# Moving loads, sums and logits between steps in a two-layer attention and mixture-of-experts kernel

## The reference

```python
x = x + attn_a(layernorm(x))   # 16 heads of 8, causal softmax attention
x = x + ffn(layernorm(x))      # 8 experts, top 2
x = x + attn_b(layernorm(x))   # 16 heads of 8, similarity scaled by norms, no mask
x = x + ffn(layernorm(x))      # the same expert weights again

def ffn(x):                    # 4096 tokens of 128
    logits = flat_x @ Wr                       # 128 -> 8
    top_vals, top_idx = top_k(logits, 2)
    combine = softmax(top_vals), one-hot over the experts
    h = silu(flat_x @ Wg[e]) * (flat_x @ Wu[e])   # 128 -> 512
    out = sum over e of combine[e] * (h @ Wd[e]) * 12 ** -0.5
```

## Time and profile before

| | us |
|---|---|
| three runs | 1113.69, 1089.67, 1102.22 |
| median | 1102.22 |
| the profiled execution, its own time | 1107.71 |
| its span from first to last instruction | 1105.3 |
| PE busy in the span | 993.8 (90%) |
| DVE busy | 771.1 (70%) |
| ACT busy | 712.6 (64%) |
| POOL busy | 542.9 (49%) |
| mean granted TensorE clock | 0.933 |

### The profile page before, as it was taken

One profiled execution on the slowest core, in us unless ns is written; L12 is line 12 of the kernel. 1 busy time (PEld: TensorE's weight loads), 2 busy tenths in 40 slices (PEclk: granted clock), 3 DMA queues, 4 the chain that ended last, 5 costly groups with the idle time before them and its releaser, 6 DMA issues.

```text
span 1105.3 us, 28185 instructions
## 1 busy us (share of the span) xinstructions
PE 993.8 (90%) x9148; PEld 701.1 (63%) x9148; DVE 771.1 (70%) x2335; ACT 712.6 (64%) x1399; POOL 542.9 (49%) x764
## 2 busy tenths in 40 slices
PE   2999999998988999998889899999988799999992
PEld 1345545554458999998734344445643589999992
DVE  4688878878677534465789989998687774443554
ACT  2367767765554566666558779999667555666661
POOL 3144445644650630255787846588416416204655
PEclk9999989999888999999959889999787799999996
DMA  5545766643223765675644434344321246667774
GB/s 154 115 109 126 178 163 140 163 109 95 61 69 90 185 168 146 159 185 149 173 102 110 108 91 89 90 100 97 70 61 45 77 112 176 158 148 170 190 189 140
DMA packets 239303, 139.86 MB, mean 127 GB/s; under 512 B 92724, under 2 KB 215352, under 8 KB 239160
## 3 DMA queue, kind: packets, MB, share of 16 engines
q1 hardware_dynamic: 230968, 121.29, 45.1%
q0 software_dynamic: 8192, 16.79, 5.2%
HBM read 87.86 MB, written 50.14 MB: 125 GB/s over the span
## 4 chain that ended last, share of the span: by engine, by line
PE 31%; DVE 10%; issue 4%; DMA 3%; SPq 3%; POOL 1%; ACT 1%; POOLq 0%; DVEq 0%; ACTq 0%
PE psS L364 5%; PE psO L330 4%; PE psT L1422 4%; PE psS L1415 4%; DVE mx L670 4%; PE psO L1436 2%; PE psN L1436 2%; PE psN L337 2%; DMA wuc<-in_L_ffn_Wu 1%; PE psM L285 1%; SPq L1509 1%; DMA xin<-xg 1%; DVE row L610 1%; PE psM L435 1%; PE psM L294 1%
## 5 line engine op out<-in xcount | busy, mean ns | idle before, releaser
L670 DVE TENSOR_REDUCE mx<-psS 128x3 f32<-128x384 f32 (+1 forms) x512 | 310.2, 618 | 94.2 <-PE psS L395 53.6
L364 PE MATMUL psS<-kst,qst 48*128 48x256 bf16 (+1 forms) x1024 | 196.4, 280 | 39.4 <-DVE mx L670 28.4
L567 ACT ACTIVATE pT<-psT,scb 128x512 f32<-128x512 f32 x256 | 193.3, 772 | 48.4 <-PE psT L372 45.5
L372 PE MATMUL psT<-qst,kst 50*128 50x256 bf16 (+1 forms) x1024 | 191.5, 274 | 7.2 <-DMA qst<-scr_m 4.8
L1298 POOL DMA_INDIRECT xg<-xn,slot x128 | 123.2, 962 | 127.5 <-DVE ysb L1483 75.0
L1462 ACT ACTIVATE sg<-psS 128x512 f32<-128x512 f32 x142 | 84.8, 597 | 145.3 <-PE psS L1415 142.7
L1422 PE MATMUL psT<-xTt,wuc 128*128 128x128 f32 x1136 | 155.1, 280 | 4.9 <-DMA wuc<-in_L_ffn_Wu 4.6
L562 ACT ACTIVATE pT<-psT 128x384 f32<-128x384 f32 x256 | 123.5, 488 | 55.1 <-PE psT L372 47.2
L1415 PE MATMUL psS<-xTt,wgc 128*128 128x128 f32 x1136 | 153.7, 279 | 4.2 <-DVE xTt L1475 4.2
L364 PEld LDWEIGHTS psS<-kst,qst 48*128 48x128 bf16 x1024 | 63.2, 96 | 139.0 <-DVE mx L670 72.3
L1488 DVE TENSOR_TENSOR hT<-sg,psT 128x512 f32<-128x512 f32 x142 | 97.0, 683 | 71.6 <-PE psT L1422 52.7
(11 more groups left out here) (228 smaller groups left out, 1621.4 us busy)
## 6 DMA issues: line engine op xcount, KB each, us to landing
wuc<-in_L_ffn_Wu SPq DMA_DIRECT2D x142, 256.0 KB
scr_part<-part SPq DMA_DIRECT2D x128, 128.0 KB, 2.4
qst<-scr_part SPq DMA_DIRECT2D x64, 192.0 KB, 3.6
kst<-scr_part SPq DMA_DIRECT2D x64, 192.0 KB, 4.6
eo<-ysb SPq DMA_DIRECT2D x142, 64.0 KB
xin<-xg SPq DMA_DIRECT2D x280, 32.0 KB
scr_part<-part SPq DMA_DIRECT2D x32, 192.0 KB, 2.1
xg<-zero SPq DMA_DIRECT2D x7, 576.0 KB, 3.7
```

The costliest lines, as they stand in the source:

```text
L364: return nc.tensor.matmul(ps[:, c0:c0 + n], q_[r64, t, q0], k_[r64, t, 0:n], start=(half == 0), stop=True, skip_group_check=True)
L372: return nc.tensor.matmul(ps[:, c0:c0 + T - q0], k_[m64, t, half * P:half * P + P], q_[m64, t, q0:T], start=(half == 0 or not L.causal), s ...
L567: nc.scalar.activation(pT[:, g % 8, 0:cols], psT[g % 2][:, 0:cols], ACT.Exp, scale=scb[r][:, 0, i:i + 1], bias=scb[r][:, 1, i:i + 1]).then ...
L670: nc.vector.tensor_reduce(mx3[:, u, 0:n, pos:pos + 1].rearrange("p a b -> p (a b)"), psS[h % 2][:, 0:kcols(L)].rearrange("p (a k) -> p a k ...
```

## The change

It does six things. (1) The down weights are issued in steps 3 to 10 of the attention of layer one instead of 4 to 11, the gate weights in steps 11 to 18 instead of 4 to 11, at the same points. (2) The logits of step 15 in layer two are issued as eight halves of two matmuls at heads 3 to 10 instead of four of four at heads 3 to 6, and DVE copies them at head 11 instead of 8. (3) The second half of the third sums of layer two's attention (step 6) moves from head 7 to head 5. (4) The statistics that stood at head 5 of step 6 move to head 9 of step 5. (5) The gathers of group 0 in layer one's experts are paced at two per tile instead of one and a half, as in layer two already. (6) Behind the tiles the additions start at 11, 15 and 19 tiles after `OWN + 1` instead of 13, 18 and 23 (in both layers), and the layer norm at 23 instead of 27 (layer one).

```diff
@@ -993,14 +993,15 @@
                                            xn[:, BASE[g] + 4 * i + m, :], ident[:])
             last.then_inc(r["T_ps"], 1)
 
-        def pe_logits(pe, n, i):
+        def pe_logits(pe, n, i, half=None):
             r = r_sem
             pe.wait_ge(r["T"], quads(n) + i + 1)
-            for m in range(4):
+            for m in range(4) if half is None else range(2 * half, 2 * half + 2):
                 k = 4 * i + m
                 last = nc.tensor.matmul(logit_bank(n, i)[:, E * k:E * k + E], xnT[i % 4][:, m * P:(m + 1) * P], wr[:],
                                         start=True, stop=True, skip_group_check=True)
-            last.then_inc(r["lg_ps"], 1)
+            if half is None or half:
+                last.then_inc(r["lg_ps"], 1)
 
         def pe_counts(pe, n):
 
@@ -1324,7 +1325,7 @@
                     pool.wait_ge(f_sem["u"], n0 + ROUTE_SLOT + 2 + pair // 2)
                 pool_scatter(pool, 2 * l + 1, pair)
             for pair in range(2 * SIZE[0]):
-                pool.wait_ge(f_sem["y"], n0 + OWN + (2 * pair // 3 if l == 0 else pair // 2) + 1)
+                pool.wait_ge(f_sem["y"], n0 + OWN + pair // 2 + 1)
                 pool_gather(pool, 2 * l, pair)
             for pair in range(2 * PARTS[1] if l == 1 else 0):
                 pool.wait_ge(f_sem["y"], n0 + OWN_A)
@@ -1608,12 +1609,12 @@
         def sp_beside(sp, j, point):
 
 
-            if 4 <= j < 4 + E and point == 3:
-                e = j - 4
+            if 3 <= j < 3 + E and point == 3:
+                e = j - 3
                 sp.dma_start(wd[:, e * HID:(e + 1) * HID].rearrange("p (k d) -> p k d", k=HB),
                              A["L0_ffn_Wd"][e].rearrange("(k p) d -> p k d", p=P)).then_inc(s_wffn, 16)
-            if 4 <= j < 4 + E and point == 1:
-                e = j - 4
+            if 11 <= j < 11 + E and point == 1:
+                e = j - 11
                 sp.dma_start(wg[:, e * HID:(e + 1) * HID], A["L0_ffn_Wg"][e]).then_inc(s_wg, 16)
             if j == 6:
                 if point == 0:
@@ -1670,8 +1671,8 @@
                 if l == 1 and j == 15:
                     if h == 3:
                         pe.wait_ge(L.s["oT"], 2 * (j - 4) + 2)
-                    if 3 <= h < 7:
-                        pe_logits(pe, n, h - 3)
+                    if 3 <= h < 11:
+                        pe_logits(pe, n, (h - 3) // 2, h % 2 == 0)
                     if h == 12:
                         pe.wait_ge(r_sem["lg"], LG_COPIES[n] + 1)
                 if l == 1 and j == 16 and h == 4:
@@ -1804,7 +1805,7 @@
             if (j, h) == (5, 5):
                 dve.wait_ge(r_sem["x"], 2 * (lo + 4))
                 dve_stats(lo, lo + 4)
-            if (j, h) == (6, 5):
+            if (j, h) == (5, 9):
                 dve.wait_ge(r_sem["x"], 2 * mid)
                 link(dve_stats(lo + 4, mid))
             if (j, h) == (6, 9):
@@ -1843,7 +1844,7 @@
         def dve_third_route(dve, j, h):
 
             n, size = 2, SIZE[0]
-            if (j, h) == (15, 8):
+            if (j, h) == (15, 11):
                 dve_logits(dve, n, 0, QUADS[0], LG_COPIES[n] + 1)
             if (j, h) == (15, 14):
                 dve_pick_top(0, 0, size)
@@ -1877,7 +1878,7 @@
                     dve.wait_ge(s_cst, 16)
                     nc.vector.memset(onesb[:], 1.0).then_inc(s_half, 1)
                     nc.vector.tensor_copy(triu[:], cst[:, CST_TRIU:CST_TRIU + P]).then_inc(s_half, 1)
-                if l == 1 and j in SUMS_AT and h in (3, 7 if j == 6 else 5):
+                if l == 1 and j in SUMS_AT and h in (3, 5):
                     dve_combine_half(dve, 0, SUMS_AT.index(j), int(h > 3))
                 if l == 1 and (j, h) == (2, 12):
                     dve_route_part(dve, 1, 2)
@@ -1916,7 +1917,7 @@
             if at in (8, 9):
                 dve_combine_0(dve, l, 2 * (at - 8))
                 dve_combine_0(dve, l, 2 * (at - 8) + 1)
-            for q, first in ((1, 13), (2, 18), (3, 23)):
+            for q, first in ((1, 11), (2, 15), (3, 19)):
                 if first <= at < first + 4:
                     dve_combine_0(dve, l, 4 * q + at - first)
             if l == 0:
@@ -1926,10 +1927,10 @@
                 if at == 11:
                     dve_ln_root(0, 4, s_lnB)
                     dve.wait_ge(s_lnB, 1)
-                if at == 27:
+                if at == 23:
                     dve.wait_ge(r_sem["x"], 2 * HALF)
-                if 27 <= at < 32:
-                    for h in (2 * (at - 27), 2 * (at - 27) + 1):
+                if 23 <= at < 28:
+                    for h in (2 * (at - 23), 2 * (at - 23) + 1):
                         dve_ln_at(dve, h, 4, HALF - 4, s_lnB, 2)
                 if k in AHEAD_XS:
                     dve_xs(dve, LB, k // (AHEAD + 2))
```

## The result

| | before | after |
|---|---|---|
| median of 22 runs | 1102.97 | 1091.09 |
| lowest and highest | 1089.67, 1113.69 | 1082.63, 1101.16 |
| the profiled execution, its own time | 1107.71 | 1082.63 |
| its span | 1105.3 | 1080.2 |
| PE busy in it | 993.8 | 974.9 |

The ratio of the times is 0.9933 with a 95% interval of 0.9906 to 0.996, so the kernel is faster, by less than 2%; by this ratio the gain is 7.4 us, between 4.4 and 10.4, and by the medians it is 11.9 us (1.1%). The ratio leaves out runs more than 1.5% above the fastest of their own kernel, here 7 of 22 before and 1 of 22 after, but that explains little of the difference, since the medians of the runs that stay, 1101.45 and 1090.46, are still 11.0 us apart. So the gain is known to a few us only.

The account below looks back on a forecast made before the run. PE was taken as the bound, its few waits paid twice, as wait and as 1.2 GHz clock. From 1107.7: -7.2 - 4.9 - 8.3 - 1.8 = -22.2, so 1085.5, plus 2.5 for a random fall: 1088 us, range 1076 to 1101.

Parts of the forecast that it names:

- Loads: Attention of layer one: moving down and gate weights shortens PE's waits for `qst` and the slow clock behind them; -7.2 us.
- the charge of 1 us: Layer one, steps 11 to 17: one short wait with its clock, caused by the gate weights' new place; 1 us on average.
- Rival B: Layer one: the round trip's delays go with the gate weights to steps 11 to 17; 1095 us, chance 0.12.
- rival D: Layer one: each of steps 11 to 17 makes PE wait as step 9 did; 1126.5 us with seven, chance 0.04.
- round trips under 2 us in steps 4 to 10: Sign of being right: in layer one's attention, storing the maxima and loading `qst` takes under 2 us.
- Sums: Layer two, steps 5 and 6: additions moved off GpSimd's large split operations, and statistics moved to step 5; -4.9 us.
- The bound for the statistics: Layer two, step 5, head 9: the four moved statistics cost between 0 and +0.9 us, +0.4 taken.
- Logits: Layer two, step 15: issued as halves between ordinary scores, the clock stays up; 28.7 us becomes 20.4, -8.3 us.
- one of two like places held: Layer one's four quads, at the same density, ran at full clock; given as reason for taking -8.3 us in layer two.
- Rival A: Layer two, step 15: the clock falls all the same, or didn't in most runs before; 1096 us, chance 0.20.
- Tail: End of layer one's experts: with the layer norm four tiles earlier, PE starts layer two at about 545.2; -1.8 us.
- what is late next: End of layer one's experts: row reduction of the second sequence, last copies and last down product need some 3.5 us from 541.7.

Follow-up runs that it names:

- loads alone: The kernel before with only the weight loads moved (down weights in steps 3 to 10, gate weights in 11 to 18): median 1101.17 us, before 1104.89; ratio 1.0015.
- filled kernel: The changed kernel with two useless matmuls of 384 columns behind each half of the logits: median 1090.24 us, before 1103.52; ratio 0.9903.

## Why the prediction was right or wrong

**The bound** was read rightly. PE's busy time went with the clock, the other engines' stayed, and both places where a wait was removed gave back more than the wait: 3.9 us for 2.7 of waits for `qst`, and 5.5 us for the 3.25 of the earlier trace rows.

**Loads: -7.2 forecast, -3.9 in steps 3 to 10, the mechanism as said.** The part for steps 3 to 10 was -8.2 and is -3.9, or -3.0 without the execution that it was read from. The step that failed is the term's size: steps 9 and 10 were priced at 6.0 us, of which 1.8 for the wait and the rest "mostly the clock". The wait comes again in every trace with these loads. The clock doesn't: PE ran at 1.2 GHz for 13.8 us of steps 3 to 10 in the profiled execution, and for 0 to 3.4 us in the four others with these loads, whose steps 9 and 10 took 33.5 to 34.4 us together and not 37.0. With the new loads they took 31.4 to 32.8.

The other part, the charge of 1 us for waits that follow the weights, was not needed: steps 11 to 17 have 2.0 us less on average, but that is within their scatter and no gain of the loads. Rival B had one trace in its favour, loads alone (128.1), but the mean of the nine with these loads (123.6) is under that of the five with the old ones, whose range is 122.9 to 126.9. Against rival D the prediction said that the old loads made PE wait in two steps; the trace before has six waits for `qst`, of 4.0 us together. Round trips behind a gate load take up to 2.5 us in the changed kernel and up to 3.4 in the others with these loads; two of the nine have waits for it in step 11 (0.7 and 0.9 us), the rest hide it. The sign "round trips under 2 us in steps 4 to 10" did not come true: 1.3 to 2.4 us in the changed kernel, and up to 3.3 in others, with no gate load near. So the gate weights were not the only thing that delays the trip; what else does wasn't looked into.

**Sums: -4.9 forecast, -5.6 in steps 5 to 7.** Right in place, cause and size, and repeated in ten traces. The bound for the statistics, 0 to +0.9, came out at less than 0.1 (step 5 takes 16.82 us, and 16.75 before).

**Logits: -8.3 forecast, 0 measured.** This is the step that made the forecast too low: "Halves at eight heads have ordinary scores between them, so that no stretch is as thin as the one before the fall". The clock held through step 15 with whole quads in two of seven traces (21.4 us twice) and fell in five; with halves it held in one of six and fell in five, once as deep as 0.66. In the trace of the changed kernel all but the last half are done at full clock. Timeline of PE there; x4 is a half, as x8 was a quad in the earlier trace rows:

```profile
766.05 0.51 PE L1001 MATMUL psO<-wr,xnT 128*128 128x8 f32 x4
...
773.91 0.51 PE L1001 MATMUL psO<-wr,xnT 128*128 128x8 f32 x4
776.76 1.02 PE L1001 MATMUL psO<-wr,xnT 128*128 128x8 f32 x4
```

So the fall came behind seven of eight halves, where it had come behind one of four quads, and the step still took 26.0 us. It came there in four of the five executions with halves in which it came at all, and these steps are shorter (25.6 to 26.0 us) than those of the five whole ones (27.1 to 28.7), but over steps 15 to 17 the fallen ones of both kinds overlap (63.4 to 70.7 and 65.6 to 67.7 us). The forecast had the price of the fall right (28.7 against 21.4 is 7.3, estimated 8.3), but not what decides it. The comparison with layer one, "one of two like places held", was wrong in another way: the places are not alike. In layer one the four quads ran at full clock in all 14 traces (0.95 to 0.96 us each), and PE even stood idle, in short waits, for 3.0 us of the 22.1 us of that step in the trace before, against 0.8 of 28.7 in step 15 of layer two. The quads are as close together in both where the clock holds. But in layer one each head of scores between them has one wide matmul more, the causal mask (first row, of before), and in layer two matmuls with a single row stand ahead of the first quad (second row):

```profile
232.18 0.28 PE L395 MATMUL psS<-trib,identb 128*128 128x256 bf16 x1
...
783.60 0.40 PE L413 MATMUL psM<-prow,ones_row 1*128 1x32 f32 x2
```

No kernel changed either of these alone, so which difference matters is not shown. What is shown is that the place which held is no evidence for the other. Rival A, which said that the clock falls all the same, had 0.20 and was what happened; its time, 1096, is 5 us too high, which is what the profiled execution stood above the median (4.7).

The Trainium skill, TensorE: Matmul & The Clock Gate, "HAM oscillation — how this bites in real kernels", which ties falls to idle gaps of PE, would have given the right sum here, 0 for this term, where the prediction had set it aside. Its reason is not what the traces show: the clock was 0.66 with PE busy 29.31 of 30.16 us.

What decides the fall from one execution to the next is open. The filled kernel kept the clock in its one trace, and that is not enough where unfilled ones keep it three times in thirteen.

**Tail: -1.8 forecast, 0 measured.** PE was forecast to start at 545.2 instead of 547.01, which is 4.1 us behind the last `hT`; it was 6.88. The root went away from the end and stayed hidden, as said. What failed is "what is late next": the prediction named the row reduction and the last copies by their durations and did not look at what the last copy itself waits for. It is the store of the tile two before: in the six traces with the new tail and no buffer of its own the last copy waits 1.6 to 2.8 us for it, and in the five with the old tail not at all or up to 0.8 us. With that wait taken away too the distance is 4.20 us in three of three, 2.1 to 2.3 less, so the prediction's 1.8 was the right size for another version of the kernel; whether it also shortens the whole time is open: two of the three kernels that have it are the best by the medians (-16.7 and -14.1), and the third is behind the changed kernel (-11.1). The faster gathers cost nothing that shows: layer one's experts take 242.5 us with the new tail and 243.1 with the old.

**The sum.** -22.2 from 1107.7 had -10.1 (logits and tail) that wasn't there, and of the -12.1 of the other two the traces show -3.9 - 5.6 = -9.5. That lies between the -7.4 us of the ratio and the -11.9 of the medians. That the forecast came out only 3.1 us off is no merit. Its sum was 10.3 us larger than the gain by the medians; it started 4.7 us above the median and added 2.5, which took back 7.2 of them. The medians of the single parts add up to -14.8 (-3.7, -9.4, -1.6, -0.1), each uncertain by a few us.

## What to carry to other kernels

Before an edit is priced by what one execution shows, ask whether the cost is there in every execution: a stall that follows from the order of instructions (step 6: 24.5 to 25.8 us in four of four) can be sized from one trace, a fall of the clock can't, and if the runs spread by 2%, a second trace of the unchanged kernel is worth more than a finer reading of the first. When work is moved away from in front of the last instruction, read what that instruction waits for beside the work, buffers and their stores included. When a like place is taken as evidence, list what stands around it in both: the mask matmuls of layer one stood in the timeline of the kernel before. And test the part that ought to be idle: it was the kernels with untouched logits that showed what the split is worth.

## What the runs showed of the hardware that was not expected

- The granted clock fell to 1.2 GHz in step 15 with PE busy 97% of the step (29.31 of 30.16 us, halves), and over the same instructions in another kernel's execution it stayed at 2.4 GHz (20.32 us busy of 21.17, halves). The step took 21.2 to 30.2 us.
- The same four quads of logits in layer one ran at 2.4 GHz in 14 of 14 traces, with PE idle, in short waits, for 3.0 of the step's 22.1 us in the trace before.
- Executions of one unchanged program on one core spread over 24 us (1089.67 to 1113.69); in the profiled pair the difference of luck, 13.2 us, was larger than the effect.
- Four additions of 128x128 on DVE took 1.12, 1.92 and 3.66 us, by how much of GpSimd's 128x512 operations they met. The 1.7 us between the last two became 5.5 us of the step, by the wait of PE and its clock.
